# Score replicas of a two-stage attention kernel: columns of wq and wk ordered by dimension then head, copies of a part loaded by one transfer, three a set

## The reference, cut to what matters

```
x  = x + cross_attention(layernorm(x), ctx)          # x: (8, 512, 256), ctx: (8, 64, 256), 16 heads of 64
n  = layernorm(x)
q, k, v = n @ wq, n @ wk, n @ wv                      # 16 heads of 16 dimensions
s  = causal(q @ k^T / 4)  for each of the 16 heads    # 512 x 512 a head
h  = n + rmsnorm(softmax(s) @ v @ wo)
dense  = h + rmsnorm((silu(h @ w1) * (h @ w3)) @ w2)
sparse = rmsnorm(top-2 of 8 experts(n))
out = x + dense + sparse
```

## Time and profile before

| | us |
|---|---|
| median of 3 runs | 1511.2 |
| lowest, highest | 1509.92, 1518.62 |
| the profiled execution, its own time | 1514.02 |
| span in that profile, first to last instruction | 1512.2 |
| PE busy in the span | 1376.5 |

### The profile page before, as it was taken

How to read it: one execution, slowest core, us unless ns; L and a number is a source line. 1 busy time by engine, 2 the same in 40 slices (tenths; PEclk the granted TensorE clock), 3 DMA queues, 4 the chain that set the end, 5 groups by cost and what they waited for, 6 DMA issues and landing times.

```text
span 1512.2 us, 22383 instructions
## 1 busy us (share of the span) xinstructions
PE 1376.5 (91%) x7229; PEld 891.4 (59%) x7230; DVE 811.6 (54%) x1652; ACT 575.4 (38%) x1214; POOL 601.4 (40%) x1051
## 2 busy tenths in 40 slices
PE   6886898999899989998999899989998789999995
PEld 6543556656665666566656665666566246666673
DVE  2625655754485358436753675366546623333348
ACT  2231553055306521641255036404540444344346
POOL 4312343253325332633254235423532435555544
PEclk8998899999999999999999999999999799999997
DMA  6054205200600060006001500240031424332245
GB/s 209 1 145 138 67 1 130 53 16 1 157 26 16 1 164 19 16 10 170 18 1 39 144 16 1 78 104 16 1 105 50 152 86 129 127 100 87 86 177 197
DMA packets 77529, 115.39 MB, mean 76 GB/s; under 512 B 24072, under 2 KB 65440, under 8 KB 74880
## 3 DMA queue, kind: packets, MB, share of 16 engines
q1 hardware_dynamic: 67120, 79.68, 18.7%
q10 hardware_dynamic: 3840, 16.78, 3.9%
q0 software_dynamic: 6480, 17.77, 3.3%
HBM read 70.22 MB, written 43.59 MB: 75 GB/s over the span
## 4 chain that ended last, share of the span: by engine, by line
PE 66%; DVE 9%; DMA 7%; POOL 5%; ACT 5%; issue 3%; SPq 3%; ACTq 0%; POOLq 0%; DVEq 0%
PE ps L1069 8%; PE ps L1033 8%; PE ps L907 7%; PE ps L888 6%; DVE nm L1519 5%; PE ps L993 5%; PE ps L955 4%; PE ps L1086 4%; PE ps L980 4%; DMA room<-parts_d 3%; PE ps L1043 3%; DMA parts_d<-room 3%; PE ps L921 2%; PE ps L1013 2%; SPq L531 2%
## 5 line engine op out<-in xcount | busy, mean ns | idle before, releaser
L1519 DVE TENSOR_REDUCE nm<-ps 128x2 f32<-128x256 f32 (+3 forms) x256 | 202.4, 819 | 103.3 <-PE ps L956 100.9
L1211 ACT ACTIVATE room<-ps 128x512 f32<-128x512 f32 x320 | 179.7, 598 | 157.0 <-PE ps L980 156.8
L1033 PE MATMUL ps<-hT,w 128*128 128x512 f32 x768 | 212.7, 421 | 0.0
L692 POOL TENSOR_SCALAR_AFFINE_SELECT room<-room 128x256 f32<-128x256 f32 (+1 forms) x320 | 121.5, 391 | 138.3 <-ACT room L1211 133.6
L955 PE MATMUL ps<-room 96*128 96x128 bf16 (+3 forms) x512 | 129.6, 315 | 44.2 <-DMA room<-parts_d 26.5
L1033 PEld LDWEIGHTS ps<-hT,w 128*128 128x128 f32 x768 | 144.7, 196 | 33.1 <-DVE hT L1547 2.0
L1235 ACT ACTIVATE room<-ps 128x512 f32<-128x512 f32 x64 | 37.2, 593 | 294.2 <-PE ps L1033 294.2
L1043 PE MATMUL ps<-w,room 128*128 128x256 f32 x512 | 137.6, 399 | 7.5 <-DVE room L1568 7.5
L1069 PE MATMUL ps<-room 128*128 x284 | 135.4, 599 | 2.4 <-ACT room L1263 2.4
L907 PE MATMUL ps<-room 128*128 128x256 f32 x512 | 123.1, 384 | 2.7 <-ACT room L1172 1.8
L888 PE MATMUL ps<-room,xnT 128*128 128x512 f32 x256 | 122.0, 601 | 0.0
(11 more groups left out here) (234 smaller groups left out, 2372.3 us busy)
## 6 DMA issues: line engine op xcount, KB each, us to landing
room<-parts_d SPq DMA_DIRECT2D x48, 256.0 KB, 5.3
room<-parts_d ACTq DMA_DIRECT2D x48, 256.0 KB, 5.7
room<-xs_d SPq DMA_DIRECT2D x71, 129.0 KB, 2.1
parts_d<-room SPq DMA_DIRECT2D x64, 128.0 KB
room<-pair_d SPq DMA_DIRECT2D x8, 1024.0 KB, 8.3
room<-in_L_ffn_ew SPq DMA_DIRECT2D x24, 256.0 KB, 5.5
xin<-in_x SPq DMA_DIRECT2D x8, 512.0 KB, 8.1
parts_d<-xnT SPq DMA_DIRECT2D x32, 128.0 KB
```

The lines of the kernel that those rows point to most:

```text
L692: done(g.affine_select(out=w, in_=w, compare_op=ALU.is_ge, fill=0.0, base=0, pattern=[[0, 2]] * (blocks - 1) + [[1, P]], channel_multiplie ...
L1033: last = mm(bank(up_banks(b, m)[i]), w[:, x, k, m * P:(m + 1) * P], hT[:, y, k, :], start=((x, y, k) == terms[0]), stop=((x, y, k) == term ...
L1211: done(fn(prob[:, u * 512:(u + 1) * 512], bank(6 + n % 2), ACT.Exp), "b_exp")
L1519: done(v.tensor_reduce(nm[:, t, 2 * hp:2 * hp + 2], pair_ps, AX.X, ALU.max, negate=True), "a_max")
```

## The change

The columns of `wq` and `wk` are reordered once, on DVE, from (head, dimension) to (dimension, head) within each half. They are first loaded into the tile of `yb`, which is free in the first walk, and copied from there with a rearranged read; PE waits for both copies. The projection's partitions then stand in the order (dimension, head), which is the order of the rows of `parts_d`, so that a store's 128 partitions go to rows at one constant stride.

The six copies of a set stand one after the other instead of interleaved (copy j on partitions 16 j to 16 j + 15), and are loaded by three transfers: one of three copies, one of two, one of one. A transfer of q reads one part as often as it has copies (part 0 three times, part 1 twice, part 2 once); a transfer of k reads parts 0, 1, 2, then 0, 1, then 0. The six products of parts are the same. The bytes are the same everywhere.

```diff
-Q_PART = (0, 0, 1, 1, 0, 2)
-K_PART = (0, 1, 0, 1, 2, 0)
+REPLICAS = ((0, 3), (3, 2), (5, 1))
...
-    q_out=96, k_out=96, rep_q=96, rep_k=96, z=1,
+    q_out=96, k_out=96, rep_q=48, rep_k=48, z=1,
...
+        w_heads = yb[:, :, :].rearrange("p t d -> p (t d)").rearrange("p (i k n) -> p i k n", i=2, k=KD)
...
-                for dst, src in ((wq, "L0_ffn_wq"), (wk, "L0_ffn_wk")):
-                    sp.dma_start(dst[:, :, :], A[src].rearrange("(k p) n -> p k n", p=P)).then_inc(p0["w_late"], 16)
+                for dst, src in ((w_heads[:, 0, :, :], "L0_ffn_wq"), (w_heads[:, 1, :, :], "L0_ffn_wk")):
+                    sp.dma_start(dst, A[src].rearrange("(k p) n -> p k n", p=P)).then_inc(p0["w_late"], 16)
...
-                            done(sp.dma_start(parts_d[i, a // 2, :, :, a % 2, :].rearrange("d h n -> h d n"), parts[i][:, a, :]), ("q_out", "k_out")[a // 2], 16)
+                            done(sp.dma_start(parts_d[i, a // 2, :, :, a % 2, :].rearrange("d h n -> (d h) n"), parts[i][:, a, :]), ("q_out", "k_out")[a // 2], 16)
...
-                    for j in range(NREP):
-                        src = parts_d[K_PART[j], 1, :, :, :, :].rearrange("d h a n -> d (h a n)")
-                        done(sp.dma_start(k_rep[j:KREP:NREP, :, :].rearrange("d h n -> d (h n)"), src), "rep_k", 16)
+                    for i, (j, n) in enumerate(REPLICAS):
+                        done(sp.dma_start(k_rep[j * HD:(j + n) * HD, :, :].rearrange("p h n -> p (h n)"), parts_d[0:n, 1, :, :, :, :].rearrange("i d h a n -> i d (h a n)")), "rep_k", 16)
...
+                                pe.wait_ge(p0["w_turned"], 2)
...
-                        for j in range(NREP):
-                            src = parts_d[Q_PART[j], 0, :, :, :, :].rearrange("d h a n -> d (h a n)")
-                            done(act.dma_start(q_rep[j:KREP:NREP, :, :].rearrange("d h n -> d (h n)"), src), "rep_q", 16)
+                        for i, (j, n) in enumerate(REPLICAS):
+                            done(act.dma_start(q_rep[j * HD:(j + n) * HD, :, :].rearrange("p h n -> p (h n)"), parts_d[i, 0, :, :, :, :].rearrange("d h a n -> d (h a n)").unsqueeze(0).to_broadcast([n, HD, H * S])), "rep_q", 16)
...
                             dve.wait_ge(p0["w_late"], 16 * 9)
+                            for i, w in enumerate((wq, wk)):
+                                v.tensor_copy(w[:, :, :].rearrange("p k (a d h) -> p (k a) d h", a=KD, d=HD),
+                                              w_heads[:, i, :, :].rearrange("p k (a h d) -> p (k a) d h", a=KD, d=HD)).then_inc(p0["w_turned"], 1)
```

More of the change, by code:

```diff
@@ L213, in xattn_ffn @@
         kv_out = [sem(f"p0_kv_out{i}") for i in range(4)]
-        p0 = {n: sem("p0_" + n) for n in ("w_first", "bias_ps", "w_early", "w_mid", "w_late", "w_up", "kv0_ps", "norms", "split_hi", "split", "ident", "const", "iota", "tr_ps", "tr_sb", "kv_ps", "kv_sb", "bk")}
+        p0 = {n: sem("p0_" + n) for n in ("w_first", "bias_ps", "w_early", "w_mid", "w_late", "w_turned", "w_up", "kv0_ps", "norms", "split_hi", "split", "ident", "const", "iota", "tr_ps", "tr_sb", "kv_ps", "kv_sb", "bk")}
         moe = {n: sem("moe_" + n) for n in ("table_step", "table", "ids_off", "ids", "ew_in", "zero", "gate", "xT_ps", "xT", "up_ps", "th", "u", "g", "gT_ps", "gT", "dn_ps", "eo")}
```

## The result

The changed kernel takes 1785.4 us (median of 4 runs, 1778.8 to 1788.6) against 1512.4 for the kernel before (median of 4). The ratio is 1.179, 95% interval 1.174 to 1.185: 273 us more. In the profiled executions the spans are 1786.8 and 1512.2 us, 274.6 apart.

The account below looks back on a forecast made before the run. PE paces the walk and its cover for the replica loads is used up. 218 (loads, walks two to eight) + 30 (first walk) + 8 (clock) = 256 on 1511.2 gave 1767 us, predicted as 1768, range 1700 to 1990.

Parts of the forecast that it names:

- The engine count: Replica loads: the side with the smaller outermost count limits the engines, so three copies get three engines and two get two.
- The same engines for all: Loads of q and k share the same lowest engines; the busiest two get 33 packets of each, 66 in all.
- The price of a packet: Replica loads on few engines: 0.70 us for each 16 KB packet, kept between 0.65 and 1.04.
- The crowded start: Rival at the loads' destination: copies on adjacent partitions crowd, packets about 1.6 us, +3 us a walk, 1536 us; chance 0.04.
- A walk: Walks two to eight: PE starts after the replica loads at 588.2 instead of 557.06, +31.1 us each, 218 for seven.
- First walk: Replica loads end near 147.8 and the context's store queues behind q's loads on ACT: +30 us (26 to 50).
- Stores: Stores to parts_d: sixteen engines, 0.35 us instead of 0.70 each, last of k landing some 2 us after issue; 0 gained.
- turned weights: First walk, once: two DVE copies of 0.69 us each before PE's first projection, hidden behind ACT, 0 to 0.4 us.
- clock: PE's lower granted clock after the stall: 1 us a walk added for uncertainty, 8 us in all.
- What is queued behind: SP's loads of the next keys, values and x behind k's loads: they land near 590, still in time, 0 us.
- All sixteen engines: Rival at the replica loads: destination's 48 and 32 partitions set the engines, all sixteen work, 1464 to 1485 us; chance 0.07.
- Crowded with sixteen engines: Rival at the replica loads: spread over the engines but crowded on adjacent partitions, about 1.6 us a packet, 1536 us; chance 0.04.

Follow-up runs that it names:

- e4: Changed kernel with the 16 dimensions outermost and the copies inside in every load, three transfers kept: 1552.7 us, ratio 1.024.
- e6: Changed kernel with k loaded by three transfers, copies outermost, and q by six single loads, both to every second row: 1657.9 us, ratio 1.094.
- e7: Changed kernel with its loads of q and k, copies outermost, going to every second row instead of adjacent rows: 1769.6 us, ratio 1.170.
- e5: Changed kernel with three loads a set of two copies each, dimensions outermost, to every third row: 1494.3 us, ratio 0.985.
- e1: Changed kernel with six single-copy loads a set again, each to 16 adjacent rows: 1595.4 us, ratio 1.052.
- e2: Changed kernel with six single-copy loads a set to every sixth row, keeping its stores and turned weights: 1491.3 us, ratio 0.983.
- e3: Kernel before with only the three-transfer loads of the change, old stores and weight order kept: 1804.6 us, ratio 1.188.
- e2b: Repeat of e2, changed kernel with six single loads a set to every sixth row: 1493.5 us, ratio 0.985.

## Why the prediction was right

The forecast was 1768 us, the range 1700 to 1990; measured 1785.

**The engine count.** Read from the stores' half share and carried over to 3 and 2, it held: three and then two engines at 26 GB/s each for most of the stall, and e4's swap of two dimensions takes 233 us off. The Trainium skill, DMA: Bandwidth & Descriptors, section "Why a DMA increments its semaphore by 16 and not by 1", says the same; the trace agrees, with 19.2% and then 12.3% of sixteen engines. The new stores reach 80% where the old ones reached 53%, 1.5 times and not the "twice" of the forecast.

**The same engines for all.** Shown by e6 against e7.

**The price of a packet.** Forecast 0.70 on average, 66 x 0.70 = 46.2 us. Measured, it is the sum of two errors of opposite sign, and that they nearly cancel is luck. Alone on its engine a packet takes 0.61, below the lower bound of 0.65; from 646 to 650 us it takes 1.76, above the upper one. Together they are 695.66 - 644.99 = 50.7 us (PE's start less 0.25, ACT's issue plus 1.49, as in the forecast) against 47.3. The crowded start was written up as a rival with 0.04 and, wrongly, as something that could hardly act in the forecast's case: the single-copy transfers use all engines in both cases.

**A walk.** Forecast +31.1, measured (1417.46 - 158.37 less 1140.04 - 122.82) / 7 = +34.6 from score product to score product. The missing 3.5 us are that start. The feed-forward ahead of the stall is 0.8 us shorter (656.74 - 643.07 against 553.21 - 538.73), as said, and that too is spent in the stall.

**First walk.** Forecast +30, measured +35.5 (37.1 from PE's first projection on). The mechanism was the one named: the context's stores on ACT's queue wait behind q's loads. ACT idles 9.4, 7.3 and 31.4 us for three of them, where the forecast had one.

**Stores, issues, turned weights, clock.** Stores land in 1.8 us, forecast "some 2", except in the sixth walk. Issues shrink to half and bring nothing. The weights cost nothing; a copy takes 0.6 us. The 8 us added for the clock were not needed. In the forecast's terms, 218 + 30 + 8 = 256 became 242 + 36 + 0, less 3 for the rest of the span: 275. That the total is only 19 us off is in part these errors offsetting each other.

**What is queued behind.** Not foreseen: SP stands 9.9 and 35.4 us at issuing keys and values, presumably because the two slow engines' queues were full, which no view shows. Nothing waited for it here; x and the keys still came in time.

**The rivals.** All sixteen engines: e5 is what that would have been with spread rows, 1494, and the forecast for it was 1480; PE still waits 3.1 us a walk there, where the rival had none. Crowded with sixteen engines: e4, 1553 against 1536, with packets of 1.73 us against about 1.6. Here the Trainium skill, SBUF — State Buffer, section "Door 1: The DMA port swizzle", bears on the size: 16 adjacent partitions would share 4 ports, four to each. The measured 2.12 us of e1 is 3.5 times the 0.61 of a packet alone, close to four; 1.09 for every sixth row and 1.73 for the sets of e4 lie in the order that it gives. What limits the spread rows to 1.09 was not separated, source or destination.

## What to carry to other kernels

Before merging transfers, write down the outermost dimension of both sides: a small one there (parts, copies, heads) costs far more than the issues that are saved, and here swapping two dimensions of the source took off 233 of the 273 us. Halving the number of transfers was worth nothing measurable (e5 against e2), while getting more engines for the stores and spreading the destination's rows were worth something. And a transfer of large packets that starts sooner holds up small ones on the same engines: ask what is still to come there before moving it.

## What the runs showed of the hardware

- A 16 KB packet from DRAM takes 0.61 us while only two engines work (changed kernel), 1.09 with sixteen engines and rows on every sixth partition (e2), 2.12 with rows on 16 adjacent ones (e1).
- A store of 1 KB packets that meets loads of 16 KB packets of the other queue on few engines lands after 24 us instead of 6.4 (e3, eight engines for the store); in the sixth walk of the changed kernel SP waits 15.6 us for stores that land in 1.8 elsewhere.
- SP itself is held for 35 us at two issues of its queue while two or three DMA engines are far behind (changed kernel, fourth walk).
- The granted clock after a stall of 39 us is back at 0.99 or 1.00 after 6 us of work, as after one of 3.9. After waits of about 2 us it sometimes falls and sometimes does not (stayed after 2.21 in e2, fell after 1.82 in e2b).
